# Causal attention with one 512-column weighting block, six probability slots, two fixed pairs of banks for products and three banks in turn for scores

## The reference

```
x  : (4, 2048, 256);  xn = layernorm(x)
q, k, v = xn @ W.T + b, 16 heads of 16
scores = q k^T / 4;  scores[k_pos > q_pos] = -inf        # causal
out    = softmax(scores) @ v;  s = out @ Wo.T + bo
g = silu(two layers of windowed attention + gated net on xn)
result = x + s * g
```

## Time and profile before

| | us |
|---|---|
| median of 3 runs | 5207.88 |
| lowest, highest | 5165.24, 5208.1 |
| the profiled execution | 5235.67 |
| its span, first to last instruction | 5233.7 |
| mean granted clock of TensorE in it | 0.915 |

### The profile page before, as it was taken

One profiled execution on the slowest core, in us unless ns is written; L12 is line 12 of the kernel. 1 busy time (PEld: TensorE's weight loads), 2 busy tenths in 40 slices (PEclk: granted clock), 3 DMA queues, 4 the chain that ended last, 5 costly groups with the idle time before them and its releaser, 6 DMA issues. The chain is left out here.

```text
span 5233.7 us, 99917 instructions
## 1 busy us (share of the span) xinstructions
PE 4816.1 (92%) x35808; PEld 3106.5 (59%) x35808; DVE 3696.0 (71%) x7557; ACT 3021.4 (58%) x6873; POOL 1338.9 (26%) x1844
## 2 busy tenths in 40 slices
PE   8599999999999999679999999997699999999986
PEld 7333333343433333267777777775477777777766
DVE  7477776776777777377777777773677777777746
ACT  3156666666666666445666666563366665656642
POOL 3111111111111111143333333330333333333300
PEclk9689888887979798789999999998799999999998
DMA  8623322222222232100000000000100000000007
GB/s 308 180 33 44 48 39 34 35 34 34 35 34 34 34 41 28 65 5 13 14 13 13 13 13 13 13 13 34 33 13 13 13 14 13 17 13 13 13 5 264
DMA packets 175716, 214.72 MB, mean 41 GB/s; under 512 B 75836, under 2 KB 126996, under 8 KB 169108
## 3 DMA queue, kind: packets, MB, share of 16 engines
q1 hardware_dynamic: 175252, 208.56, 17.5%
HBM read 124.05 MB, written 83.89 MB: 40 GB/s over the span
## 5 line engine op out<-in xcount | busy, mean ns | idle before, releaser
L595 ACT ACTIVATE a_pt<-a_ring 128x512 f32<-128x512 f32 (+3 forms) x2560 | 1209.9, 534 | 640.0 <-PE a_ring L678 623.2
L630 DVE TENSOR_REDUCE a_mx<-a_ring 128x2 f32<-128x1024 f32 (+3 forms) x1120 | 1180.2, 1068 | 463.8 <-PE a_ring L691 275.3
L720 PE MATMUL a_ot<-a_pt,a_vt 128*32 128x256 f32 (+2 forms) x8704 | 790.6, 438 | 4.4 <-issue 3.8
L691 PE MATMUL a_ring<-a_ks,a_qs 48*128 48x512 f32 (+3 forms) x2560 | 575.3, 445 | 134.4 <-DMA a_v_in<-v_d 51.4
L678 PE MATMUL a_ring<-a_qs,a_ks 49*128 49x512 f32 (+3 forms) x2560 | 637.6, 497 | 47.9 <-DMA a_qs<-a_ntb 19.2
L970 POOL TENSOR_TENSOR l_rn<-l_ssm,l_half 128x8 f32<-128x8 f32 x256 | 431.8, 1687 | 951.1 <-DVE l_ssm L1252 951.1
L678 PEld LDWEIGHTS a_ring<-a_qs,a_ks 49*128 49x128 f32 x2560 | 263.6, 201 | 558.5 <-issue 196.8
L572 POOL TENSOR_TENSOR a_gate<-a_gate 128x1 f32<-128x1 f32 x512 | 98.8, 193 | 1659.9 <-ACT a_pt L595 1655.1
L1071 ACT ACTIVATE l_pr<-l_pr,l_negm 128x256 f32<-128x256 f32 (+1 forms) x1024 | 500.7, 493 | 6.5 <-DVE l_negm L1304 6.1
L977 POOL TENSOR_TENSOR l_work<-l_work,l_rot 128x512 f32<-128x512 f32 x256 | 357.0, 1396 | 396.2 <-DVE l_work L1260 396.2
L1079 ACT ACTIVATE l_pts<-l_banks 128x512 f32<-128x512 f32 (+1 forms) x512 | 296.9, 580 | 271.7 <-PE l_banks L1581 210.0
(11 more groups left out here) (173 smaller groups left out, 9254.8 us busy)
## 6 DMA issues: line engine op xcount, KB each, us to landing
qk_d<-p_parts SPq DMA_DIRECT2D x16, 2048.0 KB, 10.1
a_qs<-qk_d SPq DMA_DIRECT2D x96, 256.0 KB, 8.9
a_ks<-qk_d SPq DMA_DIRECT2D x96, 256.0 KB, 18.9
x_d<-l_dx SPq DMA_DIRECT2D x32, 512.0 KB, 2.8
l_xt<-x_d SPq DMA_DIRECT2D x24, 513.0 KB, 3.9
p_x_in<-x SPq DMA_DIRECT2D x16, 512.0 KB, 8.6
x_d<-p_xt SPq DMA_DIRECT2D x16, 512.0 KB, 4.8
v_d<-p_vt SPq DMA_DIRECT2D x16, 512.0 KB, 10.4
```

Source lines behind the costliest of these rows:

```text
L595: act.activation(pt[:, s % NPT, j, q0:CHUNK], bank("step", k, f)[:, q0:CHUNK], ACT.Exp).then_inc(exp_done.sem, 1)
L630: r = dve.tensor_reduce(mx[:, pr, :, t, kc], ring[:, a:b + 1, 0:w], AX.X, ALU.max)
L691: mm = pe.matmul(bank("unit", n, f)[:, 0:w], qs[rows, v, pr, q0:q0 + P], ks[rows, v, pr, kc * CHUNK:kc * CHUNK + w], start=True, stop=kc < c)
L720: mm = pe.matmul(ot[j * VW:(j + 1) * VW, a:b], vt[:, v, kt, j], pt[:, s % NPT, j, a:b], start=kt == 0, stop=kt == TPC * (c + 1) - 1)
```

## The change

- `weigh` does nothing in the even slot. In the odd slot it weighs all columns from `q0` to 512 in one block.
- The probabilities have six slots (`NPT` 4 to 6), and weighting lags three steps behind the scores (`LAG` 2 to 3).
- Units, rows and outs use two fixed pairs of banks in turn (banks 0 and 1, 2 and 3). DVE's reduction is always one instruction over both banks.
- Scores use three banks in turn, one for each head: score number n goes to bank n mod 3. Before the two matmuls of a slot PE waits once, until the exponential of number 2k - 2 is done, that is the first of the two of the slot before.

```diff
-        NPT = 4
-        LAG = 2
-        NB = 7
+        NPT = 6
+        LAG = 3
+        NPAIRS = 2
+        NSC = 3
...
-        def pair_of(r):
-            return sorted((2 * r % NB, (2 * r + 1) % NB))
-
-        def bank(kind, j, f=0):
-            return ring[:, pair_of(turn_of[kind, j])[f]]
+        def score_number(g, k, f):
+
+            return g * GH * STEPS + 2 * k + f
+
+        def score_bank(g, k, f):
+            return ring[:, 2 * NPAIRS + score_number(g, k, f) % NSC]
+
+        def pair_at(g, kind, j):
+
+            return 2 * ((g * len(users) + turn_of[kind, j]) % NPAIRS)
+
+        def wait_for_scores(eng, g, k):
+
+            eng.wait_ge(exp_done.sem, exp_done.at(0, score_number(g, k, 1) - NSC + 1))
...
-                    wait_for_pair(pe, g, "step", k)
+                    wait_for_scores(pe, g, k)
                     for f in range(2):
                         rows = slice(f * HALF, f * HALF + SROWS + 1)
-                        pe.matmul(bank("step", k, f)[:, q0:CHUNK], ks[rows, u, piece, kt * P:(kt + 1) * P],
+                        pe.matmul(score_bank(g, k, f)[:, q0:CHUNK], ks[rows, u, piece, kt * P:(kt + 1) * P],
...
-                    halves = [(max(q0, a), a + CHUNK // 2) for a in (0, CHUNK // 2)]
-                    now = halves[piece:piece + 1] if kt else [(0, CHUNK)] if piece else []
...
+                    if not piece:
+                        return
...
+                    for j in range(GH):
+                        mm = pe.matmul(ot[j * VW:(j + 1) * VW, q0:CHUNK], vt[:, v, kt, j],
+                                       pt[:, s % NPT, j, q0:CHUNK],
+                                       start=kt == 0, stop=kt == TPC * (c + 1) - 1)
+                    mm.then_inc(pv_done.sem, 1)
```

More of the change, by code:

```diff
@@ L451, in attend @@
         users = []
[L452 to L453 removed]
+        body(NG // 2, unit=lambda d, n: users.append(("unit", d, n)),
              row_out=lambda d, c: users.append(("row", d, c)),
@@ new lines, in score_number @@
+        def score_number(g, k, f):
[6 more added lines that the diff above has]
+            eng.wait_ge(exp_done.sem, exp_done.at(0, score_number(g, k, 1) - NSC + 1))
+        def wait_for_pair(eng, g, kind, j):
+            q = g * len(users) + turn_of[kind, j] - NPAIRS
+            while q >= -len(users):
+                before, d, m = users[q % len(users)]
+                at = q // len(users) + d
+                if 0 <= at < NG:
+                    if before == "unit":
+                        eng.wait_ge(mm_used.sem, mm_used.at(at, m + 1))
+                    elif before == "row":
+                        eng.wait_ge(ntb_ready.sem, ntb_ready.at(at, m + 1))
+                    else:
+                        eng.wait_ge(otok_ready.sem, otok_ready.at(at, m + 1))
+                    return
+                q -= NPAIRS
@@ L607, in row_copy @@
                     act.wait_ge(m_stored[c].sem, m_stored[c].at(G - 1))
-                    act.activation(ntb[:, c], bank("row", c)[0:TASKS, 0:P], ACT.Copy).then_inc(ntb_ready.sem, 1)
+                    act.activation(ntb[:, c], ring[0:TASKS, pair_at(g, "row", c), 0:P], ACT.Copy).then_inc(ntb_ready.sem, 1)
                 body(g, step=step, raw_out=raw_out, row_copy=row_copy)
@@ L626, in unit @@
                     dve.wait_ge(mm_done.sem, mm_done.at(G, n + 1))
[L627 to L634, removed]
+                    a = pair_at(g, "unit", n)
+                    dve.tensor_reduce(mx[:, pr, :, t, kc], ring[:, a:a + 2, 0:unit_width(n)], AX.X, ALU.max)\
+                       .then_inc(mm_used.sem, 1)
                     if n == last_unit[c]:
@@ L645, in out @@
                     dve.wait_ge(otr_done.sem, otr_done.at(G, c + 1))
-                    tr = bank("out", c).rearrange("p (t h w) -> p t h w", t=TPC, h=GH)
+                    tr = ring[:, pair_at(g, "out", c)].rearrange("p (t h w) -> p t h w", t=TPC, h=GH)
                     dve.reciprocal(rden[:, :, :], tr[:, :, :, A_HD]).then_inc(rden_ready.sem, 1)
@@ L690, in unit @@
                         rows = slice(f * HALF, f * HALF + SROWS)
-                        mm = pe.matmul(bank("unit", n, f)[:, 0:w], qs[rows, v, pr, q0:q0 + P],
+                        mm = pe.matmul(ring[:, pair_at(g, "unit", n) + f, 0:w], qs[rows, v, pr, q0:q0 + P],
                                        ks[rows, v, pr, kc * CHUNK:kc * CHUNK + w],
@@ L697, in unit @@
                                 rows = slice(f * HALF, (f + 1) * HALF)
-                                mm = pe.matmul(bank("unit", n, f)[:, w - P:w], masks[rows, e, 0], masks[rows, e, 1],
+                                mm = pe.matmul(ring[:, pair_at(g, "unit", n) + f, w - P:w], masks[rows, e, 0], masks[rows, e, 1],
                                                start=False, stop=e == 1)
@@ L728, in row_out @@
                     wait_for_pair(pe, g, "row", c)
-                    pe.transpose(bank("row", c)[0:TASKS, 0:P], negm[:, c % 2],
+                    pe.transpose(ring[0:TASKS, pair_at(g, "row", c), 0:P], negm[:, c % 2],
                                  ident[:, :]).then_inc(nt_done.sem, 1)
@@ L735, in out @@
                     for t in range(TPC):
-                        mm = pe.transpose(bank("out", c)[:, t * P:(t + 1) * P],
+                        mm = pe.transpose(ring[:, pair_at(g, "out", c), t * P:(t + 1) * P],
                                           os_[:, t * P:(t + 1) * P], ident[:, :])
```

42 lines of the change are left out of this document (7 added, 35 removed).

## The result

The changed kernel is slower: 5355.92 us (median of 4 runs, 5316.76 to 5364.81) against 5196.47 for the kernel before, measured along with it (4 runs, 5165.24 to 5208.1), a ratio of 1.0286 [1.0246, 1.0326]. The medians lie 159 us apart. The two profiled executions, which the rows of before and after show, are 5364.81 and 5235.67, 129 apart. I had predicted 5400, range 5275 to 5570.

A forecast was written before the change was run, and what follows sets the result against it. PE was taken to bound the kernel (92% busy). +12.4 us a group at full clock, +10.5 after low-clock steps, gave 168 us; with 25 for the clock, 5208 + 193, rounded to 5400 us, range 5275 to 5570.

The forecast's parts named there:

- the near 300 I named: Scores of odd slots in `attend`: PE's waits for ACT's exponential would sum to near 300 us.
- Part 1: Weighting on PE: one 512-column block for two of 256 saves 0.15 us a step, 4.2 us a group.
- Part 2: Three score banks: a PE, ACT, PE loop of 1.31 us stalls PE, mostly in even slots, adding 25.1 us a group.
- The 0.66: Even slot at full clock: 0.33 + 0.33 us of PE work, scores and unit, against the loop.
- Part 3: Even slots: masks, transposes, rows and some second units hide in the stall, taking off 9.5 us a group, bounds 7 and 12.
- the forecast's 12.4 us at full clock: Sum per group in `attend`: -4.2 + 25.1 - 9.5 + 1 = +12.4 us, bounds 9.9 and 14.9.
- The bound of 106 us: Group at full clock, at chunk 3's pace of 2.66 us a step: at most 106 us, so at most 17 to hide.
- Part 4: Small terms: DVE pairs nothing, six slots and lag 0, ACT's chunk-end copy 1 us a group; SP and POOL order unchanged.
- the rival on the clock: Chunk 2's row of maxima lands in time behind longer slots, so the clock improves: 5141 us, 1.3% below; chance 0.07.
- The clock: `attend`, chunk ends and beginnings: more PE pauses add 4 us a group at 1.2 GHz, 25 us; bounds -31 and +94.
- The rival that chunk 3 would fall in its full steps: Clock falls in chunk 3's 13 full steps: 5740 us, or 5513 if in a third of the groups; chance 0.15.
- The sum: Whole kernel: 168 us from slots plus 25 from the clock, +193 us on the kernel before.

The follow-up runs named there:

- e1: Changed kernel, but scores wait for both exponentials of the slot before instead of the first: 5644.63 us, ratio 1.0809 to the kernel before.
- e7: Changed kernel with the odd slot's unit moved up into the even slot: 5289.06 us, ratio 1.0143 to the kernel before.
- e4: Kernel before with only the weighting changed to one block in the odd slot; seven-bank ring, four probability slots, lag of two kept: 5232.00 us, ratio 1.0021.
- e5: Changed kernel with the next group's loads issued in slot 10 instead of 6, behind the row of maxima: 5270.90 us, ratio 1.0108 to the kernel before.
- e6: Kernel before with the next group's loads issued in slot 10 instead of 6: 5206.08 us, ratio 0.9986.
- e9: Kernel before with one weighting block in the odd slot (ring of seven, lag of two) and loads in slot 10: 5180.12 us, ratio 0.9932.
- e10: Changed kernel with a lag of two instead of three and loads in slot 10: 5333.42 us, ratio 1.0235 to the kernel before.
- e3: Kernel before with only the banks changed (fixed pairs, three for scores); half blocks, four probability slots, lag of two kept: 5238.04 us, ratio 1.0054.
- e11: Kernel before with only the banks changed (fixed pairs, three for scores) and loads in slot 10: 5150.20 us, ratio 0.9871.

## Why the prediction was right, and where it was not

**The mechanism was right.** PE, the bound, was slowed by a loop that the change laid open; the waits name ACT, the odd slot is 1.65 us, the low-clock step 4.55 for 4.59. e1 makes the loop longer and the slot follows it; e7 adds work to the slot and it doesn't. The waits sum to 225 us, below the near 300 I named, and chunk 3 takes 45.6 us at full clock, below the 47 to 48.

**Part 1** (-4.2 us a group). The block lasts 0.99 us to the next scores, as read the earlier trace rows. But as a saving it is only paper: the block alone makes a full-clock group 4.5 us longer in the ring (e4). I had argued that the ring of seven leaves room for the exponentials; it does so mostly for scores (they wait 32.4 us for ACT in e4, 12.6 before), and e4's units wait 86.4. The sum was not hurt, since there both parts come together, but I would have predicted e4 as faster at full clock. The Trainium skill's about 2.5 ns a matmul (TensorE: Matmul & The Clock Gate, section "Back-to-back issue gap") would have made the saving an estimated 0.02 us a step; the rows after keep 0.99 for the whole block against 2 x 0.57 for the halves. The section gives the 2.5 ns for an isolated gap and says that a stream of weight loads and matmuls is spaced otherwise, so this case lies outside the rule, which I had taken to hold for every matmul, rather than against it.

**Part 2** (+25.1) was mis-sized. The loop is 1.245 us, not 1.31: ACT started 0.59 after the scores, as I took it, but from the start of the exponential to the next scores it is 0.65, not 0.74. My row for it was a unit that had waited for an exponential, and I took it to hold for scores; it was 0.09 too long for them. 28 x 0.065 = 1.8 us. The narrow slots take 1.08, 0.915 and 0.75 us (medians, 384, 256 and 128 columns), over 0.66 of work: 0.42, 0.25 and 0.09, a mean of 0.25 where I had taken 0.45 for all, 2.4 us for the 12. The 0.66 is the forecast's own figure: at full clock 45 of the 60 even slots of 256 columns held no unit and had less work than that, so the 2.4 is rough.

**Part 3** (-9.5). Masks, second units and transposes did vanish in the even slot. With the four transposes of the output in it, it lasts 1.28 us:

```profile
923.97 0.50 PE L674 MATMUL a_ring<-a_qs,a_ks 49*128 49x512 f32 x2
924.30 0.40 PE L687 MATMUL a_ring<-a_ks,a_qs 48*128 48x512 f32 x2
924.70 0.63 PE L729 MATMUL a_ring<-a_ident,a_os 128*128 128x128 f32 x4
925.25 0.50 PE L674 MATMUL a_ring<-a_qs,a_ks 49*128 49x512 f32 x2
```

The even slots with masks have a median of 1.246, with nothing beside the scores 1.238. Of the forecast's 12.4 us at full clock, 8.2 are left once Part 2 is set right; e5 against e6 measures 6.3. The 1.9 between lie in this part, in the odd narrow slots or in the rough 2.4, and inside the bounds I gave (9.5 + 1.9 = 11.4 of 12). The bound of 106 us for a group at full clock, from which I had 17 us to hide, was too low: it measures 107.8.

**Part 4** failed at "SP and POOL issue the same things in the same order", and with it "0" for the lag. The order is the same; the moment against PE is not. This wait is the term that was missing: 41 us more in the trace, 43 by what e5 gave back at full clock (39 over all runs). Worse, the rival on the clock argued the other way, that longer slots would let the row land in time. I had looked at when the row's data are ready, not at what stands ahead of it in SP's queue, and what frees that.

**The clock** was predicted to get worse (+25 us) and did not. Over all runs the time at 1.2 GHz is the same, 835 us; in the two profiled executions it is 3.1 us a group less, -18 us, 0.89 for 0.86 in `attend`. I had read the falls as following idle time of PE. The changed kernel idles more and is at 1.2 GHz no longer; e1 idles still more and falls far more; e4 and e9, in which PE idles more than in the kernel before too, spend the least time at 1.2 GHz (309 and 195 us in `attend`). So idle time alone does not order these kernels. The rival that chunk 3 would fall in its full steps happened in part: three groups have 16 to 24 us of chunk 3 at 1.2 GHz, and three more 3.4, where before the last group alone had any (4.9). For this the prediction named the Trainium skill (the same page, section "A second HAM failure mode: psum-queue depth-cycling"); the pauses it speaks of are here in every step, 0.5 us in 2.9, and in ten groups chunk 3 ran through them at 2.4 GHz.

**The sum.** Predicted 168 for the slots and 25 for the clock, 193. Measured, in 16 groups of the profiled pair: 6.4 us a group of slots, 102; the row, 43; the clock, -18; 127, for the 129 of the profiles. The slots were put 66 too high and the clock 43, the row 43 too low; the last two cancel, and that is luck. Over all runs it is 142 for slots and row together and nothing for the clock. That 5400 lies within 1% of 5356 owes something to this: a term that I left out and one that did not come stood against each other.

**What stays open** is what sets the clock's falls. Kernels with the same slots differ by 50 to 190 us of low clock in `attend` (e5 318, e10 503; e4 309, e9 195; before 513, e6 461), and this moves the time as much as the change itself. It is not only chance between runs: the four runs of e5 have clocks of 0.931 to 0.937, those of e10 0.915 to 0.919. With it stays open why late loads give the kernel before nothing and the banks alone 88 us (e3 to e11). Over all runs 25 us of these are at full clock, and 59 come from 158 us fewer at 1.2 GHz. The two profiled executions lie only 46 apart, as that of e11 is the slowest of its six.

## What to carry to other kernels

Before merging pieces of work that are spread evenly, ask what each piece covers: two half blocks cost 0.15 us a step more than one, and each covered a round trip PE, ACT, PE of 1.245 us that the one does not. A buffer count is enough only together with the spacing of the work; e3 and e4 each cost under 30 us, their combination 159. A small DMA that something waits for should not stand in a queue behind a large load: find the instruction that frees the load, since moving that by two slots moved the small one too. And compare kernels by more than their time where the clock moves: the granted clock of each run, turned into time at 1.2 GHz, took a spread of 20 us between runs down to 5.

## What the runs showed of the hardware

- The round trip from a matmul group through an exponential of 128x512 back to a matmul took 1.245 us (median of 187 slots with one unit at full clock, 10th to 90th percentile 1.239 to 1.247): 0.59 from scores to an idle ACT's start, 0.65 from there to the next scores. At 1.2 GHz 1.54. With 384, 256 and 128 columns 1.08, 0.915 and 0.75.
- Behind 13 loads issued in 6 us, the next DMA issue on SyncE's queue, a store of 128 KB, stood 19.2 to 22.5 us (14 groups each of the kernel before and the changed one) where an issue takes 0.4 without them; all that follows in that queue is late by as much.
- Each us at 1.2 GHz lengthened the run by 0.34 us (46 runs of the kernel before, granted clocks 0.911 to 0.933).
- TensorE was at 1.2 GHz while it was wholly busy, and went up to 2.4 later, when it was less so. In the chunk 3 at 1640 us, windows of 5 us:

```profile
1645.00:1650.00 5.00, 5.00 (x24) 2.26 (x26) 2.93 (x5) 1.90 (x4) 0.00 (x0) 0.50 0.13 31
...
1660.00:1665.00 5.00, 4.66 (x24) 1.61 (x22) 2.73 (x3) 2.62 (x6) 0.00 (x0) 0.54 0.01 2
1665.00:1670.00 5.00, 3.86 (x29) 1.49 (x33) 3.41 (x5) 3.41 (x8) 0.00 (x0) 1.00 0.01 2
```

The granted clock is in the third column from the right: 0.50 with PE busy for 5.00 of 5 us, and 1.00 after 1665 us with 3.86. The lower figure is in part a result of the rise, as the same matmuls take less time at 2.4 GHz; the rows show only that being busy all the time did not keep the clock up.
